# Expert lists built during the last attention batch, and a new order of the work behind the attention

## The reference, cut to what matters

```
x  = (8, 64, 256) float32, ctx = (8, 1024, 256)
x += attention(query = LN(x), keys and values = [LN(ctx), LN(x)]) @ Wo        # 16 heads of 64
x += mamba(LN(x)):  xz = LN(x) @ W_in;  x_conv = silu(conv4(x half));  z = other half
       dbc = x_conv @ x_proj;  dt = softplus(dbc[0] * dt_w + dt_b);  B, C = 16 rows each
       h_n = exp(dt * A_n) * h_n + dt * B_n * x_conv      (scan over 64 tokens, n = 0..15)
       y = (sum over n of h_n * C_n + x_conv * D) * silu(z);   out = y @ W_out + residual
x += experts(LN(x)): 8 experts, each a list of 512 of its token numbers (top_idx, repeats allowed),
       gelu(x[list] @ W1 + b1) @ W2 + b2, times combine weight, added back at the tokens
```

## Time and profile before

| | us |
|---|---|
| median of 3 runs (lowest to highest) | 828.67 (828.59 to 830.01) |
| profiled execution: its own time | 829.16 |
| profiled execution: span of the trace | 827.4 |
| x1 of pair 3 written (end of the attention) | 653.43 |
| last state of pair 3 summed by PE | 730.48 |
| busy: PE, DVE, ACT, POOL | 741.3, 503.5, 415.5, 410.5 |

### The profile page before, as it was taken

The page is one execution under the profiler, slowest core; times in us unless marked ns, Lnnn a source line. Parts: engine busy times, 40 slices in busy tenths (PEclk is TensorE's granted clock), DMA queues, the critical chain, the costliest instruction groups (busy, mean ns, idle before and its releaser), DMA issues.

```text
span 827.4 us, 14286 instructions
## 1 busy us (share of the span) xinstructions
PE 741.3 (90%) x5379; PEld 675.8 (82%) x5379; DVE 503.5 (61%) x1098; ACT 415.5 (50%) x1117; POOL 410.5 (50%) x374
## 2 busy tenths in 40 slices
PE   4979999999999999999997999999998744879996
PEld 3569999999988999999897899988988631458895
DVE  5355666557564867887686569785776396850102
ACT  2534544544345566555655465466656226714341
POOL 2817106302700499667629676784587779600000
PEclk9999999999999999999998999999999755979998
DMA  8550010020010101200210021000111119202710
GB/s 315 217 142 2 8 58 15 1 64 15 1 36 29 40 14 52 58 15 7 71 41 13 7 77 39 15 8 1 33 22 29 23 36 360 73 0 101 248 59 28
DMA packets 48839, 49.05 MB, mean 59 GB/s; under 512 B 18356, under 2 KB 43648, under 8 KB 47616
## 3 DMA queue, kind: packets, MB, share of 16 engines
q1 hardware_dynamic: 48768, 48.11, 18.8%
HBM read 43.71 MB, written 4.26 MB: 58 GB/s over the span
## 4 chain that ended last, share of the span: by engine, by line
PE 59%; DVE 15%; POOL 11%; issue 7%; ACT 5%; DMA 3%; SPq 0%; POOLq 0%; DVEq 0%; ACTq 0%
PE psum L1532 17%; PE psum L1565 13%; PE psum L1548 4%; PE psum L1913 3%; PE psum L1903 3%; POOL work L598 3%; DVE work L900 3%; PE psum L1505 3%; POOL y_sum L611 3%; POOL work L605 2%; PE psum L1485 2%; DVE rowmax L914 2%; DVE pt_lo L823 2%; PE psum L1587 2%; DMA wq_sb<-in_L_xattn_Wq_dram 2%
## 5 line engine op out<-in xcount | busy, mean ns | idle before, releaser
L1214 ACT ACTIVATE pt_hi<-psum 128x512 fp32r<-128x512 f32 (+1 forms) x192 | 87.2, 490 | 213.1 <-PE psum L1548 159.0
L1565 PE MATMUL psum<-kvn_hi,pt_hi 128*128 128x256 f32 x512 | 150.5, 294 | 2.4 <-DVE pt_hi L820 2.4
L1565 PE MATMUL psum<-kvn_hi,pt_lo 128*128 128x256 f32 x512 | 144.8, 283 | 0.0
L1565 PE MATMUL psum<-kvn_lo,pt_hi 128*128 128x256 f32 x512 | 144.7, 283 | 0.0
L914 DVE TENSOR_REDUCE rowmax<-psum 128x1 f32<-128x728 f32 x64 | 58.6, 916 | 92.8 <-PE psum L1532 92.6
L1565 PEld LDWEIGHTS psum<-kvn_hi,pt_hi 128*128 128x128 f32 x512 | 97.9, 191 | 2.7 <-DVE pt_hi L820 2.6
L1532 PE MATMUL psum<-kvt_hi,qk_hi 128*128 128x364 f32 (+1 forms) x384 | 91.6, 347 | 7.9 <-ACT prob L1334 4.3
L1565 PEld LDWEIGHTS psum<-kvn_lo,pt_hi 128*128 128x128 f32 x512 | 98.0, 191 | 0.1
L605 POOL TENSOR_TENSOR work<-work,bc 128x512 f32<-128x512 f32 x48 | 62.4, 1301 | 71.4 <-DVE work L900 71.4
L1565 PEld LDWEIGHTS psum<-kvn_hi,pt_lo 128*128 128x128 f32 x512 | 97.7, 191 | 0.0
L823 DVE TENSOR_TENSOR pt_lo<-psum,pt_hi 128x512 fp32r<-128x512 f32 x128 | 82.0, 682 | 7.0 <-ACT pt_hi L1214 6.9
(11 more groups left out here) (233 smaller groups left out, 1544.9 us busy)
## 6 DMA issues: line engine op xcount, KB each, us to landing
w<-in_L_ffn_W_dram SPq DMA_DIRECT2D x16, 1024.0 KB, 7.9
ctx_nat<-in_ctx_dram SPq DMA_DIRECT2D x8, 1024.0 KB, 5.1
bc<-dbc_keep SPq DMA_DIRECT2D x48, 128.0 KB, 4.8
q_keep<-q_t SPq DMA_DIRECT2D x1, 2048.0 KB, 8.4
q_cur<-q_keep SPq DMA_DIRECT2D x14, 128.0 KB, 3.1
wk_nat<-in_L_xattn_Wkv_dram SPq DMA_DIRECT2D x1, 1024.0 KB, 6.0
wq_sb<-in_L_xattn_Wq_dram SPq DMA_DIRECT2D x1, 1024.0 KB, 12.7
wv<-in_L_xattn_Wkv_dram SPq DMA_DIRECT2D x1, 1024.0 KB, 14.9
```

The costliest lines, as they stand in the source:

```text
L1214: act.activation(pt_hi[u][:, t0:t1, :], where[:, 0:(t1 - t0) * P].rearrange("p (t m) -> p t m", m=P), ACT.Copy)\
L1565: pe.matmul(PV, w[u][:, j, :], x_[slot][:, j, :], start=(j == 0 and w is pt_hi and x_ is kvn_hi), stop=False)
```

## The change

- **Lists in the last batch.** POOL makes the tables in step 58 (after time_x). DVE splits the token numbers and makes onetile and half of onehot at the end of step 59, the other half at the end of step 60 (4 instructions of 1024 columns instead of one of 4096). PE counts behind step 61, DVE makes valid and coef at the end of step 62, PE sums up the slots behind step 63, DVE places them and makes the first quarter of pick at the end of step 64. The second quarter is made in the drain, ahead of x1 of pair 3, the last two behind xn_t of pair 3. PE waits for the places ahead of out_proj in the drain, since the lists and out_proj share a bank. SP loads comb and b1_rows in step 58. q_cur changes places with kvt_hi[1] and kvt_lo[1] in the layout.
- **Pair 3's chain first.** DVE goes from xn_t and two quarters of pick straight to the convolution; scan_unit(left[0]) and token_scale stand behind it, scan_unit(left[1]) behind the softplus's first step, the other three scans behind scan_open(0) to (2). POOL opens left[0] to [2] at once, then coef_hl, y_skip, close left[0], open left[3], close left[1], drive 0 and 1, open left[4], drive 2, close left[2], drive 3, close left[3], drive 4, close left[4], times_gate, drives 5 to 15. ACT takes decays(left[2]) behind the dbc copy.
- **First rows of B by PE.** Four more spread matmuls (rows 0 to 3) into bank DTB, copied to b_all by ACT; SP loads 3 of the 4 parts.
- **W_out.** For pairs 0 and 1 from behind step r = 25 to step r = 26, between the logits and the turns. W_out of pair 2 goes from n = 4 to n = 8 on PE, and mixed from n = 6 to n = 11 on DVE.

The core of the diff (the bodies of the moved list functions are as before, but for the split onehot and pick):

```diff
+        LIST_TABLES, LIST_ROWS, LIST_COUNT, LIST_VALID, LIST_PLACE = (HP * (B - 1) + n for n in (2, 3, 5, 6, 7))
 # POOL, step
+                if g == LIST_TABLES:
+                    list_tables()
 # POOL, behind the attention
-            open_unit(left[0])
...
+            for u in left[:WORKS]:
+                open_unit(u)
             pool.wait_ge(r_pos, 2)
...
+            close_unit(left[0])
+            open_unit(left[3])
+            close_unit(left[1])
             pool.wait_ge(v_dtx, INLINE + 1)
-            pool.wait_ge(ld_ball, 64)
+            pool.wait_ge(m_b, 2)
             for n in range(2):
                 drive_open(n)
+            open_unit(left[4])
+            drive_open(2)
+            close_unit(left[2])
+            drive_open(3)
+            pool.wait_ge(ld_ball, 48)
             close_unit(left[3])
-            for n in range(2, DRIVES):
-                drive_open(n)
+            drive_open(4)
             close_unit(left[4])
             times_gate(INLINE - 1)
 # DVE, step
+                if g == LIST_ROWS:
+                    list_rows()
+                    for j in range(SC // 2):
+                        list_onehot(j)
+                if g == LIST_ROWS + 1:
+                    for j in range(SC // 2, SC):
+                        list_onehot(j)
+                if g == LIST_VALID:
+                    list_valid()
+                if g == LIST_PLACE + 1:
+                    list_place()
+                    first_pick(0)
 # DVE, behind the attention
-            scan_unit(left[0])
-            token_scale(last_)
-            scan_unit(left[1])
+            first_pick(2)
+            first_pick(3)
...
-            picks(0)
+            token_scale(last_)
+            scan_unit(left[0])
...
-            scan_unit(left[2])
+            scan_unit(left[1])
...
-                if n < 2:
-                    scan_unit(left[3 + n])
-                if n == 6:
+                if n < 3:
+                    scan_unit(left[2 + n])
+                if n == 11:
                     mixed(INLINE - 1, psum[:, WB, 0:C])
 # ACT
+            act.wait_ge(m_b, 1)
+            act.activation(b_all[:, 0:4, :], psum[:, DTB, :].rearrange("p (n m) -> p n m", m=P), ACT.Copy)\
+                .then_inc(m_b, 1)
 # PE, before_turns (removed from after_turns, where it stood at r = 25)
+                t = pair_at(g, 26)
+                if t is not None and t < INLINE - 1:
+                    pe.wait_ge(v_y, t + 1)
+                    pe.wait_ge(s_mlo, misc_count(b + 1, 2) if b + 1 < B else MISC * B)
+                    w_out(zs[t % 2], MB[:, 0:C]).then_inc(v_yo, 1)
 # PE, after_turns
+                if g == LIST_COUNT:
+                    list_counts()
+                if g == LIST_PLACE:
+                    list_slots()
```

More of the change, by code:

```diff
@@ L269, in perceiver_kernel @@
         ld_bc = [sem(f"ld_bc{i}") for i in range(ROWS)]
-        m_pad, m_tap, m_dt0, m_dta, m_dec, m_drv, m_scan, m_c, m_rd, m_acc, m_zs, m_out = (sem("m_" + n) for n in (
-            "pad tap dt0 dta dec drv scan c rd acc zs out").split())
+        m_pad, m_tap, m_dt0, m_dta, m_dec, m_drv, m_scan, m_b, m_c, m_rd, m_acc, m_zs, m_out = (sem("m_" + n) for n in (
+            "pad tap dt0 dta dec drv scan b c rd acc zs out").split())
         r_idx, r_tab, r_oh, r_cnt, r_val, r_pre, r_pos, r_b1, r_b1e = (sem("r_" + n) for n in (
@@ L486, in _ @@
             sp.wait_ge(st_dbc, 16 * TT)
-            for q in range(4):
+            for q in range(1, 4):
                 part = dbc_keep[INLINE % 2, 1 + 4 * q:5 + 4 * q, :].rearrange("(a n) p -> a n p", a=1)
@@ L720, in _ @@
                 .then_inc(f_hl, 1)
-            close_unit(left[2])
-            open_unit(left[4])
+            pool.wait_ge(v_xc, INLINE + DT)
+            pool.tensor_tensor(y_skip[:], xc[:], dvec[:, 3, :].unsqueeze(2).to_broadcast((P, DT, P)), ALU.mult)\
+                .then_inc(v_y0, 1)
             def drive_open(n):
@@ new lines, in list_onehot, with list_valid @@
+            def list_onehot(j):
+                part = slice(j * E, (j + 1) * E)
+                dve.tensor_tensor(onehot[:, part, :], iota_f[:].unsqueeze(1).to_broadcast((P, E, P)),
+                                  place_f[:, part].unsqueeze(2).to_broadcast((P, E, P)), ALU.is_equal)\
+                    .then_inc(r_oh, 1)
+            def list_valid():
+                dve.wait_ge(r_cnt, 1)
+                counts = psum[:, JB, 0:TT * E].rearrange("p (e t) -> p t e", t=TT)
+                dve.tensor_scalar(valid[:], counts, 1.0, None, ALU.min).then_inc(r_val, 1)
+                dve.wait_ge(ld_comb, 32)
+                dve.tensor_tensor(coef[:], counts, comb[:], ALU.mult).then_inc(r_val, 1)
@@ new lines, in list_place @@
+            def list_place():
+                dve.wait_ge(r_pre, 1)
+                link(dve.tensor_tensor(slot_of[:], psum[:, JB, 64:64 + TT * E].rearrange("p (t e) -> p t e", e=E),
+                                       valid[:], ALU.mult))
+                dve.tensor_scalar(slot_of[:], slot_of[:], 1.0, None, ALU.subtract).then_inc(r_pos, 1)
+                link(dve.tensor_reduce(most[:], psum[:, JB, 128:128 + E], X, ALU.max))
+                dve.tensor_copy(most_i[:], most[:]).then_inc(r_pos, 1)
+                dve.wait_ge(r_pos, 2)
@@ L909, in step, with first_pick @@
+            def first_pick(t):
+                last = dve.tensor_tensor(pick[:, t, :, :], iota_f[:].unsqueeze(1).to_broadcast((P, E, P)),
+                                         slot_of[:, t, :].unsqueeze(2).to_broadcast((P, E, P)), ALU.is_equal)
+                if t == TT - 1:
+                    last.then_inc(f_pick, 1)
             def step(b, slot, hp, live, more, pair):
@@ L1384, in _ @@
             act.activation(dbc[:], psum[0:NX, DB[0], 0:P], ACT.Copy).then_inc(v_dbs, 1)
+            decays(left[2])
             act.wait_ge(v_dl, INLINE + 1)
@@ L1672, in free_bank, with list_counts, list_slots @@
                     pe.wait_ge(m_out, t + 1)
+            def list_counts():
+                pe.wait_ge(r_oh, SC)
+                for e in range(E):
+                    for j in range(SC):
+                        last = pe.matmul(psum[:, JB, e * TT:(e + 1) * TT], onehot[:, j * E + e, :],
+                                         onetile[:, j * E + e, :], start=(j == 0), stop=(j == SC - 1))
+                last.then_inc(r_cnt, 1)
+            def list_slots():
+                pe.wait_ge(r_val, 2)
+                upto = psum[:, JB, 64:64 + TT * E].rearrange("p (t e) -> p t e", e=E)
+                pe.matmul(upto, upto_ones[:], valid[:], start=True, stop=False)
+                for t in range(TT - 1):
+                    pe.matmul(upto[:, t + 1:, :], ones[:], valid[:, t:t + 1, :].to_broadcast((P, TT - 1 - t, E)),
+                              start=False, stop=(t == TT - 2))
+                for t in range(TT):
+                    last = pe.matmul(psum[:, JB, 128:128 + E], ones[:], valid[:, t, :], start=(t == 0),
+                                     stop=(t == TT - 1))
+                last.then_inc(r_pre, 1)
             def after_turns(b, hp, now):
@@ L1797, in _ @@
             spread_out(0)
+            pe.wait_ge(v_dl, INLINE + 1)
+            for j in range(4):
+                last = spread(psum[:, DTB, j * P:(j + 1) * P], 1 + j)
+            last.then_inc(m_b, 1)
             spread_out(1)
```

93 lines of the change are left out of this document (36 added, 57 removed).

## The result

| | before | after |
|---|---|---|
| median of 10 runs each (lowest to highest), us | 829.63 (828.04 to 833.91) | 825.29 (823.83 to 827.54) |
| ratio of the two, 95% interval | | 0.9936 (0.9916 to 0.9956) |
| span of the profiled execution, us | 827.4 | 825.1 |
| x1 of pair 3 written, start of the row | 653.01 | 659.51 |
| from there to the end of the last sum of pair 3 | 77.4 | 68.7 |

What follows compares the result with a forecast made beforehand. It took PE to bound the attention's steps, with POOL nearly as full, and nothing behind them to be PE-bound. -4.5 + 8 - 11.4 = -7.9 from 829.16 gave 821.3, stated as 821; range 813.5 to 828.

Steps and rivals of the forecast that it cites:

- Part 1: W_out at the front of step r = 26: pair 0's turns start 4.95 us earlier, gain carried; -4.5 us, bounds 0 to 5.
- Part 2: Lists in attention steps 58 to 64 delay the POOL and PE chains up to the drain's last scan; +8 us, bounds 3 to 12.
- DVE, end of step 59 ... 4.6 us, to 608.3: Four small instructions (0.5), onetile (0.2) and two quarters (2.15), each with up to one POOL multiply ahead, make step 60's maxima late.
- The tables' 1.7 us: POOL's tables behind time_x in step 58 make unit closing and opening, and with them DVE's scans, 1.7 us later.
- The quarters of pick in the drain: Two quarters of pick lie in DVE's waits before 648.31 and 653.01: nothing, or 1.1 us each if that cover is gone.
- Part 3: Behind the attention: earlier taps, first drive and scan 5, and no wait for W_out of pair 2; -11.4 us, bounds -7 to -15.5.
- From scan 5 on ... -2.7: In the last scans, two read buffers and an addition three states later hide W_out of pair 2; its 2.67 us wait goes.
- First rows of B by PE: Ahead of drive 0: without PE's rows the loads land at about t = 23; worth 0 to 1 us, taken as 0.
- rival B: Behind the attention, POOL's rest of pair 2 sets every state to scan 5; tail gives only 7 us, 825.2; chance 0.15.
- Rival C: PE's clock, once down in step 60, stays down; with two such steps +4 us, 832.7; chance 0.10.
- Rival A: The lists cost little where they are put in the attention, 3 to 4 us; total 815.7; chance 0.22.
- the prediction's rule: A POOL multiply and a DVE instruction with two SBUF inputs do not run together; a quarter of onehot alone takes 1.07 us.

## Why the prediction was right, and where its terms were off

- **Part 1** (forecast -4.5): the mechanism is shown, at its place, by the timeline and by the kernel with this edit alone. Its size was 6.1 to step 58: I had taken off 0.45 for a wait that did not come, and missed 1.1 that went between the turns of step 45 and step 58; where these were waits was not followed up.
- **Part 2** (forecast +8, bounds 3 to 12): +10.9. The step that was mis-sized is "DVE, end of step 59 ... 4.6 us, to 608.3": on the clock of before the list work took 8.1 us, since not only the quarters but also the small instructions waited for a POOL multiply (0.95, 1.16 and, for onetile, 1.33 us, where I had 0.7 for all five), and PE stood for 7.7 instead of 5. The lowered clock came as forecast; the logits of step 61 took 5.2 us instead of 3.3, inside my "up to 3 more". Against the kernel with W_out alone (A 67.0) the lists cost 12.2, my upper bound. The tables' 1.7 us, which I had as a term, are worth nothing (tables ahead of time_x). The quarters of pick in the drain, costed at nothing, took 2.11 and 1.91 us, not 1.07 each; they did lie in waits of DVE, but the second left only 0.17 us ahead of x1 where it was 2.00.
- **Part 3** (forecast -11.4): -8.8. Up to scan_open(5) every mark is within 0.6 us. The step that failed is "From scan 5 on ... -2.7", that two read buffers and three states hide W_out of pair 2. PE's side job of the same state stood behind W_out, ACT's copy of it behind that, and ACT's next decays behind the copy:

```profile
714.52 1.89 PE L1676 MATMUL psum<-wout,zs 128*128 128x256 f32 x8
716.25 0.60 PE L1879 MATMUL psum<-ident,coef 128*8 128x128 f32 x4
```

```profile
716.89 0.59 ACT L1445 ACTIVATE coef_t<-psum 8x512 f32<-8x512 f32 x1 [2.58 <-PE psum L1879]
717.38 1.22 ACT L1460 ACTIVATE psum<-dts_l,a_neg 128x126 f32<-128x126 f32 x4
```

so scan_open(12) waits 1.16 at 718.63, behind the 0.89 for W_out itself. (The kernel before had 0.77 at this state and the kernel with W_out at n = 12 has 0.76, so some 0.4 of the 1.16 is W_out's.) At n = 8 another 1.34 went where PE's clock had fallen to the lower level in its 2.5 us wait before scan 5's sum (0.67 on average in the window from 703 to 706; that this is the cause is read from the trace, not tried). 0.9, 0.4 and 1.3 make up the 2.7 that were to be gained: about half is W_out's, half the wait at n = 8.
- **First rows of B by PE**, a step inside part 3 that I took as worth 0 to 1: 5.8 us of T (all rows of B by DMA). The forecast of the store was right, that of the loads behind it 5 us too early. The sum did not suffer, since the rows by PE were in it.
- **The sum.** -6.1 + 10.9 - 8.8 = -4.0, against -7.9; two profiled executions differ by 2.3 in span, since the changed kernel's was already 1.8 us later at the maxima of step 44, before any edit acts (in the profiled executions of the other kernels this mark lies between 442.3 and 446.4). All three parts came out 1.6 to 2.9 us off, and that part 1 erred the other way than parts 2 and 3 kept the sum within 4 us: this much is luck. The forecast's own band for the likeliest case (-11 to -4.5) holds the measured -5.3; by the medians it is a near miss, -4.3, and 825.29 is outside 817.7 to 824.2 and at rival B's 825.2. But B's mechanism did not come: the tail gave 8.8 and not 7, and less than forecast for another reason, since drive 0 and scan 5 were on time. Rival C did not come: the clock was back at 1.00 in every window from 617 to 629. Rival A is refuted by the doubled quarters.
- What the forecast did not see is the balance: the change's lists and order were worth nothing together (W_out alone 0.9925, all 0.9936), and 12 us lay in placing the same work elsewhere.

## What to carry to other kernels

Work moved from a serial tail into a stage whose engines are full costs what it waits for there, not what its columns take: here a quarter of 1.07 us of DVE work took 2.0 to 2.3 beside a busy POOL, and a second one in the same step cost PE its clock as well. Put at most what fits the step's slack into each step, and look for the instruction behind it that the bounding engine needs. And in a loop where every engine has one turn per state, a 1.9 us guest on PE was paid at every place tried, at least in part, since something of the loop (a read, the side job's copy, the last sum) stood behind it each time.

## What was unexpected of the hardware

- The store of dbc (16.5 KB) and the loads that wait for it: 1.33 us from issue to issue in the kernel before (678.16 to 679.49), 3.9 in the changed one and 4.0 with all rows by DMA. In the latter two the last load of unit rows had been issued within 1 us ahead of the store in the same queue, before it was more than 5; that this is the cause is argued, not tried.
- DVE's small instructions on 32 columns, 0.17 us alone, took 0.95 and 1.16 us when POOL was inside a multiply, and ended within 0.05 us of POOL's instruction (599.81 and 599.78, 601.10 and 601.05 in the changed kernel). They have one input tensor each: the waiting was not limited to instructions with two, as the prediction's rule had it.
